# Another order of the pieces of a turn on TensorE, ScalarE, VectorE and GpSimd, and one wait more in the value products

## What is computed

```python
x = layernorm(x + L0_attn(x))   # linear attention with RoPE, a 5-tap convolution of v, an output gate
x = layernorm(x + L0_ffn(x))    # base matrix + the best of four low-rank adapters (a routed choice)
x = layernorm(x + L1_attn(x))   # causal softmax attention, one head of 128
x = layernorm(x + L1_ffn(x))    # 16 experts of width 64, grouped top-4 routing, and a shared expert
```

## Time and profile before

| what | value |
|---|---|
| median of three runs (lowest to highest) | 723.95 us (723.59 to 724.94) |
| the profiled execution's own time | 723.07 us |
| its span, first to last instruction | 721.2 us |
| busy: PE, DVE, ACT, POOL | 91%, 83%, 66%, 43% of the span |
| turns 3 to 15, each | 39.7 to 39.9 us |
| fill before turn 3, drain from turn 16 | 104.5 us, 99.1 us |

### The profile page before, as it was taken

One profiled execution on the slowest core, in us unless ns is written; L12 is line 12 of the kernel. 1 busy time (PEld: TensorE's weight loads), 2 busy tenths in 40 slices (PEclk: granted clock), 3 DMA queues, 4 the chain that ended last, 5 costly groups with the idle time before them and its releaser, 6 DMA issues.

```text
span 721.2 us, 11796 instructions
## 1 busy us (share of the span) xinstructions
PE 657.6 (91%) x3632; PEld 504.0 (70%) x3632; DVE 598.1 (83%) x1892; ACT 473.0 (66%) x966; POOL 312.7 (43%) x857
## 2 busy tenths in 40 slices
PE   3557679999999999999999999999999999999994
PEld 2445558687877878786878778786868778666552
DVE  1555678989899998989898999989898989877672
ACT  2152548576867868686777778586867777676533
POOL 1324444463535455464545354554645353433211
PEclk9876989999999999999999999999999999999998
DMA  6000000000101010100101010101001000000000
GB/s 226 15 1 15 1 16 1 15 1 2 30 1 30 1 31 1 31 1 0 30 1 30 1 30 1 30 1 30 1 1 30 1 16 2 15 1 15 1 15 29
DMA packets 18686, 12.69 MB, mean 18 GB/s; under 512 B 704, under 2 KB 18240, under 8 KB 18368
## 3 DMA queue, kind: packets, MB, share of 16 engines
q1 hardware_dynamic: 18624, 11.95, 5.4%
HBM read 7.75 MB, written 4.19 MB: 17 GB/s over the span
## 4 chain that ended last, share of the span: by engine, by line
PE 76%; DVE 13%; issue 3%; POOL 3%; ACT 3%; DMA 1%; DVEq 0%; SPq 0%; ACTq 0%; POOLq 0%
PE bank L578 14%; PE bank L359 10%; PE bank L368 10%; PE bank L361 9%; PE bank L360 9%; DVE gu L1100 3%; PE bank L475 2%; PE bank L500 2%; PE bank L507 2%; DVE stats L911 2%; PE bank L419 2%; PE bank L438 2%; PE bank L463 2%; PE bank L545 2%; DVE hid L1110 1%
## 5 line engine op out<-in xcount | busy, mean ns | idle before, releaser
L766 ACT ACTIVATE silu<-bank 128x512 f32<-128x512 f32 x144 | 86.4, 600 | 106.6 <-PE bank L361 104.2
L359 PE MATMUL bank<-x3T_hi,w_hi 128*128 128x512 f32 x288 | 143.1, 497 | 8.2 <-DVE gu L1100 7.9
L578 PE MATMUL bank<-hid,whole 128*128 128x512 f32 x288 | 145.9, 598 | 0.1
L360 PE MATMUL bank<-x3T_lo,w_hi 128*128 128x512 f32 x288 | 114.1, 396 | 0.0
L361 PE MATMUL bank<-x3T_hi,w_lo 128*128 128x512 f32 x288 | 114.0, 396 | 0.0
L1100 DVE TENSOR_TENSOR gu<-silu,bank 128x512 f32<-128x512 f32 x128 | 86.5, 676 | 13.9 <-PE bank L361 11.4
L1110 DVE TENSOR_TENSOR hid<-gu,bank 128x512 f32<-128x512 f32 x128 | 86.8, 678 | 4.4 <-PE bank L578 2.0
L1193 POOL TENSOR_TENSOR oT<-mixT,gT 128x512 f32<-128x512 f32 x16 | 20.6, 1287 | 147.7 <-DVE mixT L904 147.7
L359 PEld LDWEIGHTS bank<-x3T_hi,w_hi 128*128 128x128 f32 x288 | 54.3, 189 | 38.1 <-DVE gu L1100 16.9
L1201 POOL TENSOR_TENSOR moment<-stats 128x4 f32<-128x4 f32 x192 | 33.9, 209 | 94.5 <-DVE stats L911 76.6
L360 PEld LDWEIGHTS bank<-x3T_lo,w_hi 128*128 128x128 f32 x288 | 54.4, 189 | 18.7 <-issue 12.5
(11 more groups left out here) (214 smaller groups left out, 1654.5 us busy)
## 6 DMA issues: line engine op xcount, KB each, us to landing
x_in<-x SPq DMA_DIRECT2D x16, 256.0 KB, 3.0
out<-x SPq DMA_DIRECT2D x16, 256.0 KB, 2.2
whole<-w_whole SPq DMA_DIRECT2D x1, 1198.5 KB, 5.4
w_raw<-w SPq DMA_DIRECT2D x1, 1152.0 KB
w_raw<-w SPq DMA_DIRECT2D x1, 546.0 KB, 6.7
whole<-w_whole SPq DMA_DIRECT2D x16, 32.0 KB
whole<-w_whole SPq DMA_DIRECT2D x1, 64.0 KB
```

The source lines that it names most:

```text
L359: mm(out, wh, mh, start=True, stop=False)
L360: mm(out, wh, ml, start=False, stop=False)
L578: mm(YB[:], whole[:, a:a + P], hid[:, c % 2], start=c == 0, stop=c == CHUNKS).then_inc(p_w2.sem, 1)
L766: fn(silu[:, c % 2], GB[:], ACT.Silu).then_inc(a_silu.sem, 1)
```

## The change

The pieces are called in another order in `turn` on PE, ACT, DVE and POOL, and `c_value` waits for the transposed x2 in both halves. No computation is added or removed. The wait, and a line or two of each list (the rest are moves of such lines):

```diff
             def c_value(n, half):
+                pe.wait_ge(a_xT[2].sem, a_xT[2].at(n))
                 if half == 1:
                     pe.wait_ge(a_cq.sem, a_cq.at(n))
...
                 if a: a_qk(i)
-                if d: d_down(i - 3, 0)
                 if c: c_av(i - 2)
                 if b: b_xT(i - 1)
                 if a: a_g_(i)
+                if d: d_down(i - 3, 0)
...
+                if a: x0_hi(i)
                 if d: d_silu(i - 3, 0)
-                if a: x0_hi(i)
-                if second(i): split_late()
...
                 if d: d_silu(i - 3, 3)
+                if second(i): split_late()
...
                 if b: copy_xT(i - 1, 2, B0)
+                if b: c_query(i - 1)
                 if e: e_norm(i - 4)
-                if b: c_query(i - 1)
...
+                if b: c_value(i - 1, 0)
                 if second(i): split_late()
-                if b: c_value(i - 1, 0)
                 if b: c_value(i - 1, 1)
...
-                if e: ln_of(3, i - 4)
                 if a: a_rope(i)
                 if c: ln_of(2, i - 2)
                 if b: b_norm(i - 1)
+                if e: ln_of(3, i - 4)
```

More of the change, by code:

```diff
@@ L598, in turn @@
                 if a: a_g_(i)
+                if d: d_down(i - 3, 0)
+                if b: b_small(i - 1)
                 if a: a_v_(i)
-                if b: b_small(i - 1)
-                if a: a_qT_(i)
                 if d: d_hidden(i - 3, 1 - odd, 2)
@@ L605, in turn @@
                 if d: d_down(i - 3, 1)
+                if a: a_qT_(i)
                 if d: d_hidden(i - 3, 1 - odd, 4)
                 if c: r_xT(i - 2, odd)
+                if d: d_down(i - 3, 2)
                 if a: a_num_(i)
-                if d: d_down(i - 3, 2)
                 if d: d_hidden(i - 3, 1 - odd, 5)
+                if c: r_gate(i - 2)
                 if b: b_dnT(i - 1)
                 if d: d_down(i - 3, 3)
-                if c: r_gate(i - 2)
-                if d: d_down(i - 3, 4)
                 if a: a_aT(i)
                 if b: b_up(i - 1)
+                if d: d_down(i - 3, 4)
                 if d: d_hidden(i - 3, 1 - odd, 6)
@@ L785, in turn @@
                 if a: a_v_(i)
-                if a: a_qT_(i)
                 if d: d_silu(i - 3, 2)
                 if d: d_silu(i - 3, 3)
+                if second(i): split_late()
                 if c: c_norm(i - 2, odd)
                 if d: d_silu(i - 3, 4)
+                if a: a_qT_(i)
                 if b: b_exp(i - 1)
                 if c: r_hi(i - 2, odd)
+                if c: r_exp(i - 2)
+                if b: b_dnT(i - 1)
                 if d: d_silu(i - 3, 5)
-                if b: b_dnT(i - 1)
-                if c: r_exp(i - 2)
                 if d: d_silu(i - 3, 6)
@@ L800, in turn @@
                 if b: copy_xT(i - 1, 2, B0)
+                if b: c_query(i - 1)
                 if e: e_norm(i - 4)
-                if b: c_query(i - 1)
+                if first_turn(i): fold_keys()
                 if d: d_y(i - 3)
-                if first_turn(i): fold_keys()
             for i in range(turns):
@@ L1120, in turn @@
                 a, b, c, d, e = live(i), live(i - 1), live(i - 2), live(i - 3), live(i - 4)
-                if b: a_layer_norm(i - 1)
                 if c: c_max(i - 2)
@@ L1125, in turn @@
                 if e: d_res(i - 4, odd)
+                if b: a_layer_norm(i - 1)
                 if a: a_rope(i)
@@ L1128, in turn @@
                 if d: d_gu(i - 3, 1)
+                if b: b_norm(i - 1, 0)
                 if d: d_hid(i - 3, 1)
@@ L1131, in turn @@
                 if d: d_gu(i - 3, 2)
-                if b: b_norm(i - 1, 0)
                 if b: b_norm(i - 1, 1)
+                if a: a_kv(i)
                 if d: d_hid(i - 3, 2)
+                if a: conv_tap(i, 2)
                 if d: d_gu(i - 3, 3)
-                if a: a_kv(i)
-                if d: d_hid(i - 3, 3)
-                if a: conv_tap(i, 2)
                 if b: b_logits(i - 1)
                 if b: b_first(i - 1)
+                if d: d_hid(i - 3, 3)
                 if d: d_gu(i - 3, 4)
+                if a: conv_tap(i, 3)
                 if b: b_weigh(i - 1)
-                if d: d_hid(i - 3, 4)
-                if a: conv_tap(i, 3)
                 if a: a_den(i)
-                if d: d_gu(i - 3, 5)
                 if a: a_att(i)
@@ L1149, in turn @@
                 if c: r_groups(i - 2, 0)
+                if d: d_hid(i - 3, 4)
+                if c: r_groups(i - 2, 1)
+                if c: r_groups(i - 2, 2)
                 if a: a_mix(i)
-                if c: r_groups(i - 2, 1)
+                if c: r_groups(i - 2, 3)
+                if d: d_gu(i - 3, 5)
+                if b: b_res(i - 1)
                 if d: d_hid(i - 3, 5)
-                if b: b_res(i - 1)
                 if d: d_gu(i - 3, 6)
@@ L1156, in turn @@
                 if a: a_res(i, odd)
-                if c: r_groups(i - 2, 2)
-                if c: r_groups(i - 2, 3)
                 if d: d_gu(i - 3, 7)
```

## The result

The changed kernel takes 715.26 us (median of four runs, 713.38 to 717.12) against 723.77 for the kernel before beside it: a ratio of 0.9881, interval 0.9852 to 0.991. Run again, later and beside the experiments, it took 716.25 (six runs, 714.3 to 717.18), ratio 0.9884 (0.9856 to 0.9912). The forecast was 717.4. The profiled execution takes 715.15 us, its span is 713.4; against the 723.07 and 721.2 of before both are 7.9 and 7.8 less.

A forecast was written before the change was run, and what follows sets the result against it. PE was taken to set the pace in turns 3 to 15. A turn gains 0.73 + 0.08 - 0.15 - 0.10 = 0.56, 13 turns 7.3, less 0.7 in the fill: 6.6 us, so 717.4 us from the median; range 711.9 to 722.

The forecast's parts named there:

- A: Last chunk's U half: four small routing operations leave the place ahead of `gu` of chunk 7, gaining 0.73 us a turn.
- C: `d_down` ahead of the transpose of `att` on PE: `att` is ready earlier than its reader, gaining 0.08 us a turn.
- D: `c_av` on PE loses the `d_down` that covered its wait for `probT`: cost 0.15 us a turn, between 0 and 0.86.
- E: `gu` of chunk 5 moves back on DVE, 0.05 us ahead of chunk 6's U half: cost 0.10 a turn, bounds 0 and 0.65.
- The fill: Turn 1: `split_late` between the halves of `c_value`'s bias delays the second sequence's scores; cost 0.7 us, between 0 and 2.75.
- The drain: Turns 16 and 17: `r_exp` ahead of the sixth SiLU against part of a gain; 0, bounds 0.73 either way each.
- Two of its signs: Expected in the trace: `gu` of chunk 5 ending within 0.1 us of its U half; `c_av` waiting 0.1 to 0.3 for `probT`.
- `cross`: Rival: behind `mixT`, `cross` meets POOL's `oT` and is held; a turn loses 0.64, E is 1.3, 733 us; chance 0.12.
- DVE would be the bound: Rival: DVE slips half a us from the rope to chunk 5's `gu`; 0.01 gained a turn, 724.5 us; chance 0.14.
- POOL's power: Rival: moved layer norm 3's 1.02 us operation on POOL holds a two-input DVE operation; 730.7 us; chance 0.04.
- The wait in `c_value`: Added wait on PE: costs nothing, as `c_project` ahead already waits for the same copy; 0.16 a turn if cover were lost.
- the two table loads fewer: On ACT: priced at nothing, as ACT has 10 us idle a turn; pays only where ACT is waited for.

The follow-up runs named there:

- e1_groups_alone: Kernel before, with only the four small routing operations on DVE moved to their changed places, around `mixT`: 722.58 us, ratio 0.9972.
- e6_down0_back: Changed kernel with the first `d_down` on PE back ahead of `c_av`: 718.61 us, ratio 0.9901.
- e5_cross_late: Changed kernel with parts 2 and 3 of the routing groups, all four operations, behind `mixT`: 725.43 us, ratio 1.0016.
- e9_groups_and_gu5: Kernel before, with the four small routing operations moved and `gu` of chunk 5 put behind `cross` on DVE: 722.6 us, ratio 0.9976.
- e2_groups_back: Changed kernel with parts 2 and 3 of the routing groups back ahead of `gu` of chunk 7: 721.84 us, ratio 0.9955.
- e4_split_ahead: Changed kernel with `split_late` on DVE back ahead of both halves of the bias: 715.02 us, ratio 0.9872.
- e13_split_and_turn2: Changed kernel with the old lists in turn 2 alone and `split_late` on DVE ahead of the bias: 713.46 us, ratio 0.9847.

## Why the prediction was right, point by point

**What bounds the kernel**: as read. PE sets the pace of the steady turn, and what an order can give there is the time in which PE stands.

**A, gain 0.73**: measured 0.73 in the last chunk, and 0.08 more that I had not seen: the bias of `cv`, at the end of DVE's turn, also comes earlier, and the first chunk of the next turn no longer runs into a wait for it. But the words "nothing else is late there next" hold only for that end of the turn. By itself the move gains 0.19 (e1_groups_alone), since the same operations make `oT` late.

**C, gain 0.08**: 0.09. **D, cost 0.15**: 0.08. The reason given for a value near the lower end, the earlier copy of x0, was tested and is worth 0.57. What I had not counted is that the `d_down` covers another copy in its new place.

**E, cost 0.10**: 0 in the changed kernel, 0.33 where only the two moves of DVE are made. The sum of DVE's operations was right to 0.1 us there. What was wrong is "it is due at the same place": in that run A's own gain, most of it in the first chunk, brings PE there 0.11 earlier. What I left out of the changed kernel is the gain in DVE's own order, 0.32, for the most part by operations that no longer stand right behind the one whose result they read, and 0.16 by `c_av`, which is earlier by the whole `d_down`. With the `d_down` back (e6_down0_back) E stays at 0. Nor did I see that `gu` of chunk 5 has to be moved for A to work: it stood as a cost of its own.

So a steady turn gains 0.73 + 0.08 + 0.09 - 0.08 = 0.82, where 0.56 was forecast; 0.81 is measured.

**The fill, cost 0.7**: this is the step that failed. Its words are "Now they delay the second sequence's scores, with nothing else in flight to hide it", and a quarter of 2.75. Turns 1 and 2 lost 1.56 us and turn 3 another 0.52, and turn 3 began at 106.47, past the 106 that I had set as proof against it. The mechanism named is real, but its price goes by a race with `x0T_lo`: 0.1 to 0.6 us of waiting in the six profiles in which it is won (0.45 in the first), 2.2 in the two in which it is lost. And there is a part that I had not priced at all: the new order of turn 2, in which pieces stand ahead of `mixT` with no experts to run beside them. The two overlap, but turn 2's order is the larger: taken back it gives 0.8 us of turns 1 to 3 by itself and 1.7 where `split_late` is ahead, and `split_late` gives 0.2 by itself and 1.1 where turn 2 is as before (one profile of each; the changed kernel's own two differ by 0.4). **The drain, 0**: 0.7 gained.

Summed over the profiled execution, 7.9 us less than before instead of 6.6: turns 3 to 15 gave 9.2 and not 7.3 (+1.9), turns 0 to 2 cost 2.0 and not 0.7 (-1.3, of which 0.4 in turn 0), the drain gave 0.7 and not 0. That the forecast is so near is luck in part: errors of opposite sign stand in it. Two of its signs also came out otherwise, both to the good: `gu` of chunk 5 ends 0.36 ahead of its U half and not within 0.1, and `c_av` costs 0.08 and not 0.1 to 0.3.

**The rivals.** `cross` was 0.09 ahead of `oT` and not 0.06; the point from which it decides lies between 0.07 ahead (`pair_hi` of e5_cross_late) and the 0.02 behind of the earlier trace rows. The price of 1.3 a turn was twice too high: 0.69, as there were 0.36 us of room and not 0.05. That DVE would be the bound is what e9_groups_and_gu5 shows, at 39.45 a turn. No wait of PE in a steady turn leads to POOL's power, and `proj_sq`, which began 0.17 us into one, took its 0.29. The wait in `c_value` and the two table loads fewer were not tried; the value products take 0.45 and 0.44 in a turn before and after.

## What to carry to other kernels

When an operation is moved away from one wait, follow it to its new place and ask which wait ends next there: here the move of four small operations gained 0.19 us a turn alone, 0.39 with one other piece, and 0.81 in all with the moves on four engines around it. In a full list it also counts what stands right behind what: the same operations of DVE took 0.3 us less in an order in which fewer of them read the result of the one just ahead. An order that is tuned for the full turns of a pipeline should be held against the turns in which it fills: there the pieces that were moved to cover each other stand alone, and an order of its own in one of 20 turns, with one piece put back in another, gave 2.8 us. Where two engines exclude each other, read the lead in the trace and not only the order of the lists: about a tenth of a us decided 0.7 us a turn, and in the fill it went either way from one execution to the next.

## What the runs showed of the hardware

An operation with a single tensor input can be held too: `penalty` in turn 2 of the changed kernel, a TENSOR_SCALAR of 128x16 that takes 0.18 in the full turn, began 0.05 us after POOL's `x3T_lo` and was held for 1.24 (POOL, then DVE; in turn 2 of e2_groups_back it began 0.49 behind and took 0.87):

```profile
99.31 1.26 POOL L1242 TENSOR_TENSOR x3T_lo<-x3T,x3T_hi 128x512 fp32r<-128x512 f32 x1
99.36 1.24 DVE L1026 TENSOR_SCALAR penalty<-g_rank 128x16 f32<-128x16 f32 x1
```

The clock adds to a stand: behind the wait for x2 in turn 2, PE runs at the lower of its two levels (0.50) until the granted clock rises, at 104 before and at 108 after (windows of 1 us):

```profile
103.00:104.00 1.00, 1.00 (x6) 0.79 (x4) 0.93 (x4) 0.88 (x2) 0.00 (x0) 0.50 0.00 0
104.00:105.00 1.00, 1.00 (x9) 1.00 (x10) 0.72 (x3) 1.00 (x1) 0.00 (x0) 0.99 0.00 0
...
107.00:108.00 1.00, 1.00 (x5) 0.90 (x4) 0.14 (x1) 0.43 (x1) 0.00 (x0) 0.50 0.06 16
108.00:109.00 1.00, 1.00 (x5) 0.66 (x4) 0.00 (x0) 0.98 (x3) 0.20 (x1) 0.98 0.00 0
```

PE had stood 3.59 us for x2 before and 4.36 after. The value products of turn 2 then take 2.27 us after and 1.77 before, and the first 1.6 us of turn 3 lie at the lower level too, while before the higher one came 0.5 us ahead of it. That makes 0.5 us in turn 2 and, by the 40.2 against the 39.74 of the kernels that have the old turn 2, 0.5 in turn 3: some 1 us of the fill's loss lies at the lower level. The length of the stand alone doesn't order the cases: it is 3.50 in e4_split_ahead, whose turn 3 also takes 40.24, and 3.75 in e13_split_and_turn2, whose turn 3 takes 39.75. What decides it stays open.
